# B times input for seven of sixteen states by ScalarE scales and TensorE transposes, and C rows by DMA

## The chip, the cores and the metric

One core of one Trainium2 chip runs the whole program. The metric is the device time of one execution in microseconds (us); the median of several executions is compared. A profile of one execution gives a time for every instruction; it has a span (first to last instruction) and a time of its own, which is a little longer.

## What is computed

Three layers on `x` (8 batches of 256 rows with 128 columns): half an expert layer (8 experts, the best two of each row), a Mamba block, and half an expert layer again, each with a layer norm ahead. The change is in the Mamba block:

```python
gate  = silu(x_conv) * z
delta = softplus(gate @ W_dt.T + b_dt)
BC    = gate @ W_xproj.T
B_p, C_p = (BC[..., :n], BC[..., n:])                 # n = 16 states
delta_A   = exp(einsum('bld,dn->bldn', delta, -exp(A_log)))
delta_B_x = einsum('bld,bln,bld->bldn', delta, B_p, gate)
h = a * h + bx                                        # scan over the 256 rows of a batch
y = einsum('lbdn,bln->bld', hs, C_p)
```

So for each state n: a decay, an input (delta times gate times B of the state), a scan along the rows, a product with C of the state, and a sum over the states.

## The kernel before

The 128 channels lie on the partitions. The 2048 rows are four groups of 512 (two batches each, `GT` = 512); a group runs through 16 states, so the stage has 64 states, numbered k = 16 q + n. Every engine has a queue of its own and does it strictly in order; the order is written out by hand, with semaphores between the engines.

For one state before the change:

- TensorE spreads row n of B over all partitions into PSUM bank n % 2 (`spread_b`, L965, a matmul with a one-hot column), five states ahead, and row n of C into bank 2 + n % 2 (`spread_c`, L971), four states ahead.
- ScalarE makes the decay exp(delta times -A) into PSUM bank 4 + n % 2 (`decay`, L677) one state ahead, and copies the C row into SBUF (`copy_c`, L717).
- VectorE multiplies the B row with delta times gate (`b_times_input`, L1378, the tile called `gate` holds that product by then), one state ahead of the scan, then scans (`scan`, L1385).
- POOL multiplies the scan with the C row (`step`, L507) into a ring of four, and TensorE adds the result into the PSUM bank of y with an identity matmul (`sum_states`, L981). Scan k waits for product k - 4 of POOL, which waits for sum k - 8.

Within the 16 states of group q the next group is prepared: TensorE makes the B and C product behind sum 2 (`through_w_bc`, L933) and the delta product behind sum 5 (`through_w_dt`, L937); ScalarE copies B and C at its step 5 (`bc_hi`, L636), does abs and relu of delta at steps 7 and 8, exp and log at 10 and 11 (L639 to L650); VectorE adds the low part of B and C at step 6 (`bc_lo`, L1339); POOL adds to delta behind its product 11 (`add_delta`, L487; it waits for the logarithm, `log_done`, ahead of product 11) and multiplies gate with delta behind product 12 (`gate_delta`, L491, which raises `dg_ready`). The first B product of the next group on VectorE waits for `dg_ready`. VectorE also sums y of the group before at step 2 (`y_add`, L1371).

In the last group nothing is prepared; TensorE's queue has the old rows of the next router (`old_rows`, L1042, two matmuls with 8 columns at each of states 4 to 11) and, at state 13, the y transposes and the output gate (`y_rows`, L1027, `through_out_gate`, L1048).

SP issues DMAs; between the loads of the first expert layer's rows and the stores ahead of the second expert layer it has none.

## Time and profile before

| | us |
|---|---|
| runs | 446.58, 448.4, 448.22; median 448.22 |
| the profiled execution | 445.89, span 444.1 |
| state stage, first B product to the last sum of y | 169.42 to 290.16: 120.7 |
| busy over the span: TensorE, VectorE, POOL, ScalarE | 393.5, 311.4, 279.0, 229.6 |

Times in the rows are us from the span's start. PE is TensorE, PEld its weight loads, DVE VectorE, ACT ScalarE, POOL GpSimd, SP the engine that issues DMAs. L numbers are lines of the kernel. An engine's operations overlap a little: the distance between two starts says what one costs, the length says when its result is there.

### The profile page before, as it was taken

What the parts mean: (1) busy time and instruction counts of PE and PEld (TensorE: products, weight loads), DVE (VectorE), ACT (ScalarE), POOL (GpSimd) and SP (SyncE); (2) the same over time, 40 slices, a digit from 0 to 9 for tenths busy, and PEclk for the clock granted to TensorE, in tenths of its full rate; (3) what the DMA queues carried; (4) which work ended last, traced back from release to release, by engine and by line L of the source; (5) the groups of instructions that cost most, each with busy time, mean ns of one, the idle gap of its engine ahead of it and who ended that gap; (6) DMA issues with size and microseconds to landing.
All of it is one profiled execution on the core that took longest, in us unless ns stands there. A gap on an engine that the chain in (4) does not pass through costs nothing. (4 is left out here: it accounts for less than half of the span.)

```text
span 444.1 us, 10062 instructions
## 1 busy us (share of the span) xinstructions
PE 393.5 (89%) x2636; PEld 309.0 (70%) x2637; DVE 311.4 (70%) x820; ACT 229.6 (52%) x544; POOL 279.0 (63%) x263
## 2 busy tenths in 40 slices
PE   8689999999996898989979889992799999999970
PEld 5349999999996343534334345671499999999970
DVE  4765555555557867999999999989655555555565
ACT  3635444444443248686776866534564444444410
POOL 2147777777634152788687796775477767777340
PEclk9869999999999899999999999998799999999995
DMA  7952111111230300000000000001111111112305
GB/s 255 370 184 85 52 48 45 41 53 44 45 115 6 95 0 0 1 2 0 1 0 0 0 1 1 1 1 48 66 52 48 49 41 48 47 44 45 110 22 190
DMA packets 12254, 25.05 MB, mean 56 GB/s; under 512 B 3517, under 2 KB 5060, under 8 KB 11968
## 3 DMA queue, kind: packets, MB, share of 16 engines
q1 hardware_dynamic: 7232, 15.38, 10.0%
q0 software_dynamic: 4992, 9.32, 7.7%
q8 instruction: 12, 0.20, 0.2%
q14 instruction: 18, 0.15, 0.1%
HBM read 17.34 MB, written 8.26 MB: 58 GB/s over the span
## 5 line engine op out<-in xcount | busy, mean ns | idle before, releaser
L853 PE MATMUL ps<-xT,w_now 128*128 128x128 f32 x1248 | 152.6, 275 | 0.9 <-ACT xT L590 0.7
L853 PEld LDWEIGHTS ps<-xT,w_now 128*128 128x128 f32 x1248 | 145.8, 192 | 1.8 <-ACT xT L590 1.2
L1276 DVE TENSOR_TENSOR hidden<-ps,hidden 128x256 f32<-128x256 f32 x156 | 58.9, 419 | 87.0 <-PE ps L853 87.0
L460 POOL DMA_INDIRECT expert_rows<-ysb,put_i x78 | 81.4, 1044 | 46.0 <-DVE ysb L1284 33.3
L607 ACT ACTIVATE hidden<-ps 128x256 f32<-128x256 f32 x156 | 51.4, 381 | 110.2 <-PE ps L853 110.1
L452 POOL DMA_INDIRECT xg<-xn_rows,get_i x78 | 80.5, 1032 | 41.5 <-issue 13.4
L512 POOL TENSOR_TENSOR shared<-ring_space,shared 128x512 f32<-128x512 f32 x64 | 81.7, 1289 | 32.5 <-DVE ring_space L1392 18.0
L878 PE MATMUL ps<-w_down,hidden 128*128 x624 | 81.9, 275 | 0.0
L878 PEld LDWEIGHTS ps<-w_down,hidden 128*128 128x128 f32 x624 | 75.7, 192 | 0.0
L987 PE MATMUL ps<-shared,consts 128*128 128x512 f32 x128 | 68.3, 616 | 8.0 <-POOL shared L512 7.8
L723 ACT COPY shared<-ps 128x512 f32<-128x512 f32 x64 | 37.5, 587 | 31.0 <-DVE ring_space L1392 17.8
L600 ACT COPY w_now<-w_gate_up 128x512 f32 x78 | 48.1, 620 | 7.2 <-issue 7.2
L681 ACT ACTIVATE ps<-xn,neg_a 128x510 f32<-128x510 f32 (+1 forms) x64 | 44.7, 699 | 0.2 <-DVE xn L1367 0.2
L968 PE MATMUL ps<-bc,sel_r 96*128 96x512 f32 (+1 forms) x64 | 43.6, 687 | 0.9 <-ACT xnT L546 0.8
L1392 DVE TENSOR_TENSOR_SCAN ring_space<-ps,ring_space 128x512 f32<-128x512 f32 x32 | 38.6, 1210 | 0.8 <-DVE ring_space L1382 0.8
L1392 DVE TENSOR_TENSOR_SCAN ring_space<-ps,hidden 128x512 f32<-128x512 f32 x32 | 38.3, 1205 | 0.0
L1268 DVE COPY w_now<-w_gate_up 128x512 f32 x78 | 34.8, 448 | 3.1 <-issue 2.9
L987 PEld LDWEIGHTS ps<-shared,consts 128*128 128x128 f32 x128 | 21.5, 189 | 19.6 <-POOL shared L512 16.5
L1284 DVE COPY ysb<-ps 128x128 f32<-128x128 f32 x78 | 22.7, 292 | 15.6 <-PE ps L878 8.7
L779 PE MATMUL ps<-ones_b 128*128 128x512 bf16 x84 | 27.7, 496 | 2.6 <-POOL xnT L417 1.3
L424 POOL TENSOR_TENSOR rstd<-var_e,neg_half 128x4 f32<-128x4 f32 (+1 forms) x10 | 12.1, 1206 | 28.0 <-DVE var_e L1129 28.0
L974 PE MATMUL ps<-bc,sel_r 96*128 96x512 f32 (+1 forms) x64 | 27.1, 427 | 2.8 <-ACT shared L723 2.3
(172 smaller groups left out, 397.2 us busy)
## 6 DMA issues: line engine op xcount, KB each, us to landing
w_gate_up<-in_experts SPq DMA_DIRECT2D x8, 512.0 KB, 8.2
xn_rows<-xn SPq DMA_DIRECT2D x8, 256.0 KB, 3.9
w_down<-in_experts SPq DMA_DIRECT2D x1, 2048.0 KB, 11.1
ring_space<-expert_rows SPq DMA_DIRECT2D x2, 1024.0 KB, 5.2
xg<-xn_rows,get_i POOLq DMA_INDIRECT x78, 2.6
expert_rows<-ysb,put_i POOLq DMA_INDIRECT x78, 2.3
x<-in_x_rows SPq DMA_DIRECT2D x4, 256.0 KB, 4.7
gate<-expert_rows SPq DMA_DIRECT2D x3, 256.0 KB, 3.4
```

The costliest lines, as they stand in the source:

```text
L452: pool.indirect_dma_start(out=xg[:, r, :], out_offset=None, in_=xn_dram[l], in_offset=bass.IndirectOffsetOnAxis(ap=get_i[:, t:t + 1].bitca ...
L460: pool.indirect_dma_start(out=y_dram[l], in_=ysb[:, t % RING, :], in_offset=None, out_offset=bass.IndirectOffsetOnAxis(ap=put_i[:, t:t + 1 ...
L512: pool.tensor_tensor(hc[:, n % 4, :], hs[:, n % 4, :], c_row[:, n % 4, :], ALU.mult).then_inc(hc_ready, 1)
L600: nc.scalar.copy(w_now[:, slot % W_SLOTS, 0:F], flat_gate_up[:, bass.ds(at, F)]).then_inc(w_gate_ready, 1)
L607: nc.scalar.activation(gelu[:, slot % 2, half], ps[:, GATE_BANK[slot % 2], half], ACT.Gelu).then_inc(gelu_done, 1)
L681: nc.scalar.activation(to, from_delta, ACT.Exp, scale=neg_a[:, n:n + 1]).then_inc(decay_ready, 1)
L853: m = pe.matmul(ps[:, bank, f * P:(f + 1) * P], w_now[:, slot % W_SLOTS, first + f * P:first + (f + 1) * P], xT[:, slot % X_SLOTS, :], sta ...
L878: m = pe.matmul(ps[:, RESULT_BANK[slot % 2], 0:D], hact[:, slot % H_SLOTS, f * P:(f + 1) * P], flat_down[:, bass.ds(expert + f * D, D)], s ...
L968: pe.matmul(ps[:, n % 2, :], sel_r[0:BCR, n:n + 1].to_broadcast([BCR, P]), bc[0:BCR, bass.ds(q * GT, GT)], start=True, stop=True).then_inc ...
L987: pe.matmul(y_bank(q), ident, hc[:, n % 4, :], start=(n == 0), stop=(n == N - 1)).then_inc(hc_summed, 1)
L1276: dve.tensor_tensor(hact[:, slot % H_SLOTS, half], ps[:, UP_BANK[slot % 2], half], gelu[:, slot % 2, half], ALU.mult).then_inc(hact_done, 1)
L1392: dve.tensor_tensor_scan(hs[:, n % 4, :], ps[:, DECAY_BANK + n % 2, :], bx[n % 4], 0.0, ALU.mult, ALU.add).then_inc(h_ready, 1)
```

## The change

Of the 16 states of a group, nine (`PLAIN`: 0, 1, 2, 4, 6, 8, 10, 12, 14) keep their way: spread of B, product on VectorE, decay into PSUM. But B now has one PSUM bank instead of two (`B_BANK`; state 1 of group 0 alone uses `PREP_BANK`). The other seven (`TURNED`: 3, 5, 7, 9, 11, 13, 15) go another way. Once a group TensorE transposes delta times gate (`turn_u`, behind sum 12, after `dg_ready`) and computes B with rows on the partitions (`turned_b`, behind the B and C product); ScalarE copies both to SBUF (`copy_u`, `copy_bt`). For each turned state ScalarE scales the four blocks of the turned input by the column of turned B (`scale_u`), and TensorE transposes the four results back into PSUM (`turn_scaled`), from which the scan reads them; the decay of a turned state goes to SBUF. ScalarE makes decays and scalings three states ahead instead of one (`ACT_LAG`), and TensorE turns four ahead (`TURN_LAG`).

C is no longer spread and copied by TensorE and ScalarE: ScalarE copies the last 32 of 96 rows of the B and C product to SBUF (`c_sb`), SP stores the 16 C rows of a group to HBM (`store_c`) and loads each row to all 128 partitions by a broadcast DMA into a ring of eight (`c_rows`), seven states ahead; POOL waits for the landing instead of for ScalarE.

The groups 1 and 2 were a hardware loop on each engine; on TensorE and ScalarE they are now written out. The core of the diff:

```diff
+B_LAG, TURN_LAG, ACT_LAG = 5, 4, 3
+TURNED = 3, 5, 7, 9, 11, 13, 15
+PLAIN = tuple(n for n in range(N) if n not in TURNED)
+B_BANK, PREP_BANK, S_BANK = 0, 1, 2
...
+            def c_rows():
+                store_c(0)
+                for q in range(GROUPS):
+                    sp.wait_ge(c_stored, 16 * (q + 1))
+                    for n in range(N):
+                        k = q * N + n
+                        if n == C_STORE_AT and q + 1 < GROUPS:
+                            store_c(q + 1)
...
+                        if k >= C_RING:
+                            sp.wait_ge(hc_ready, k - C_RING + 1)
+                        sp.dma_start(c_row[k % C_RING], c_dram[k:k + 1].to_broadcast([P, GT])
+                                     ).then_inc(c_loaded[k % C_RING], 16)
...
+                def scale_u(q, n):
+                    act.wait_ge(u_copied, q + 1)
+                    act.wait_ge(bt_copied, q + 1)
...
+                    for c in range(GC):
+                        i = nc.scalar.activation(scaled[:, side(n), c, :], ut[:, q % 2, c, :], ACT.Copy, scale=bt[:, q % 2, c, n:n + 1])
+                    i.then_inc(scaled_ready, 1)
+
+                def make_ready(q, n):
+                    if n in TURNED:
+                        scale_u(q, n)
+                    decay(q, n)
...
                     for n in range(N):
                         before(q, n)
-                        copy_c(q * N + n, n, False, False)
-                        decay(q + (n + 1) // N, (n + 1) % N)
+                        make_ready(q + (n + ACT_LAG) // N, (n + ACT_LAG) % N)
                         prepare(q, n)
...
+                def spread_b(q, n, bank=B_BANK):
+                    if past(plain_before(q, n)):
+                        pe.wait_ge(bx_ready, plain_before(q, n) - (bank != B_BANK))
...
+                def turn_scaled(q, n):
+                    pe.wait_ge(scaled_ready, turned_before(q, n) + 1)
...
+                    for c in range(GC):
+                        t = pe.transpose(ps[:, S_BANK + side(n), c * P:(c + 1) * P], scaled[:, side(n), c, :], ident)
+                    t.then_inc(scaled_turned, 1)
+
+                def feed(q, n):
+                    if (n + B_LAG) % N in PLAIN:
+                        spread_b(q + (n + B_LAG) // N, (n + B_LAG) % N)
+                    if (n + TURN_LAG) % N in TURNED:
+                        turn_scaled(q + (n + TURN_LAG) // N, (n + TURN_LAG) % N)
...
                         through_w_bc(q + 1, next_bank(q))
+                        pe.wait_ge(u_copied, q + 1)
+                        turned_b(q + 1, ps[:, PREP_BANK, :])
...
+                    if n == PE_U_AT:
+                        pe.wait_ge(bt_copied, q + 2)
+                        turn_u(q + 1)
...
+                    else:
+                        dve.wait_ge(scaled_turned, turned_before(q, n) + 1)
+                        dve.wait_ge(sb_decay_ready, turned_before(q, n) + 1)
+                        kept, added = sb_decay[:, side(n), :], ps[:, S_BANK + side(n), :]
```

## Rows read from the trace of the kernel before

**Rows 1.** Windows by group: stretch, length, busy by engine, PEclk, DMA share, GB/s.
```profile
169.42:200.91 31.49, 28.29 (x75) 12.99 (x73) 29.59 (x35) 24.81 (x43) 19.67 (x16) 1.00 0.00 1
200.91:229.97 29.06, 25.84 (x68) 11.75 (x68) 28.76 (x35) 21.30 (x38) 22.57 (x19) 1.00 0.00 0
229.97:259.17 29.20, 25.80 (x69) 11.75 (x68) 28.92 (x34) 21.24 (x38) 22.84 (x19) 1.00 0.00 0
259.17:290.16 30.99, 29.92 (x120) 17.78 (x120) 30.85 (x51) 18.41 (x32) 24.90 (x20) 1.00 0.00 1
```

**Rows 2.** Timeline of VectorE: start, length, engine, line, operation, tiles, count.
```profile
208.96 0.66 DVE L1382 TENSOR_TENSOR ring_space<-ps,gate 128x512 f32<-128x512 f32 x1
209.54 1.21 DVE L1392 TENSOR_TENSOR_SCAN ring_space<-ps,ring_space 128x512 f32<-128x512 f32 x1
...
212.97 0.67 DVE L1342 TENSOR_TENSOR bc<-ps,bc  x1
...
227.60 2.33 DVE L1392 TENSOR_TENSOR_SCAN ring_space<-ps,hidden 128x512 f32<-128x512 f32 x2
...
290.16 0.68 DVE L1375 TENSOR_TENSOR gate<-ps,xnT 128x512 f32<-128x512 f32 x1
```

**Rows 3.** Timeline of POOL, products 11 and 12 of group 1, with idle time before.
```profile
224.37 1.30 POOL L512 TENSOR_TENSOR shared<-ring_space,shared 128x512 f32<-128x512 f32 x1 [1.04 <-ACT hidden L650]
225.61 1.29 POOL L488 TENSOR_TENSOR xn<-xn,hidden 128x512 f32 x1
227.15 1.28 POOL L512 TENSOR_TENSOR shared<-ring_space,shared 128x512 f32<-128x512 f32 x1 [0.26 <-DVE ring_space L1392]
228.38 1.28 POOL L492 TENSOR_TENSOR gate<-gate,xn  x1
```

**Rows 4.** Timeline of ScalarE in group 1, from its step 7 to the logarithm.
```profile
216.05 0.59 ACT L723 COPY shared<-ps 128x512 f32<-128x512 f32 x1 [2.30 <-PE ps L938]
216.53 0.70 ACT L681 ACTIVATE ps<-xn,neg_a 128x510 f32 x1
217.16 0.68 ACT L640 ACTIVATE hidden<-ps,vectors 128x512 f32 x1
...
223.51 0.62 ACT L650 ACTIVATE hidden<-hidden 128x512 f32<-128x512 f32 x1
```

**Rows 5.** Timeline of ScalarE, two forms of 128 columns elsewhere in the program.
```profile
294.49 4.24 ACT L566 ACTIVATE shared<-ps,yrstd 128x128 f32<-128x128 f32 x16 [7.56 <-PE ps L1036]
...
309.16 1.65 ACT L557 ACTIVATE xn<-x,shift,rstd 128x128 f32<-128x128 f32 x4 [2.27 <-POOL shift L430]
```

**Rows 6.** Timeline of TensorE: records in a run (a float32 matmul is two records).
```profile
172.65 1.88 PE L930 MATMUL ps<-xnT,mats 128*128 128x512 f32 x4
...
203.00 1.02 PE L987 MATMUL ps<-shared,consts 128*128 128x512 f32 x2
...
204.08 0.39 PE L974 MATMUL ps<-bc,sel_r 96*128 96x512 f32 x1
204.31 1.02 PE L987 MATMUL ps<-shared,consts 128*128 128x512 f32 x2
...
285.20 1.05 PE L1031 MATMUL ps<-consts,gate 128*128 128x128 f32 x8
286.09 0.96 PE L1050 MATMUL ps<-out_gate,gate 128*128 128x8 f32 x8
```

**Rows 7.** Timeline of ScalarE ahead of group 0 and at its decay 2.
```profile
164.07 0.69 ACT L640 ACTIVATE hidden<-ps,vectors 128x512 f32<-128x512 f32 x1 [0.28 <-PE ps L938]
...
174.85 0.69 ACT L681 ACTIVATE ps<-xn,neg_a 128x510 f32<-128x510 f32 x1
```

**Rows 8.** The page: DMA rate in 40 slices; issues, count, KB, us to landing.
```profile
GB/s 255 370 184 85 52 48 45 41 53 44 45 115 6 95 0 0 1 2 0 1 0 0 0 1 1 1 1 48 66 52 48 49 41 48 47 44 45 110 22 190
...
gate<-expert_rows SPq DMA_DIRECT2D x3, 256.0 KB, 3.4
```

**Rows 9.** Windows, columns as in rows 1: a stretch ahead of the second expert layer.
```profile
305.00:310.00 5.00, 0.00 (x0) 0.00 (x0) 4.69 (x28) 2.73 (x8) 2.12 (x4) 0.65 0.28 107
```

More of the change, by code:

```diff
@@ L104, with plain_before, turned_before, side @@
 assert HEAD + LOOPS * UNROLL == NT - TAIL and UNROLL % RING == 0 and UNROLL % 6 == 0
+def plain_before(q, n):
+    return q * len(PLAIN) + sum(m < n for m in PLAIN)
+def turned_before(q, n):
+    return q * len(TURNED) + sum(m < n for m in TURNED)
+def side(n):
+    return (PLAIN.index(n) if n in PLAIN else TURNED.index(n)) % 2
+def earlier_on_side(q, n):
+    kind = PLAIN if n in PLAIN else TURNED
+    for m in range(n - 1, n - 1 - N, -1):
+        if m % N in kind and side(m % N) == side(n):
+            if m < 0 and isinstance(q, int) and q == 0:
+                return None
+            return q * N + m
 def past(value):
@@ L266, in macaron_block @@
         silu = shared[:, 4 * GT:6 * GT].rearrange("p (r t) -> p r t", r=2)
-        c_row = shared[:, 4 * GT:8 * GT].rearrange("p (r t) -> p r t", r=4)
-        bc = sb("bc", [BCR, T], F32R)
+        w_rows = w_now[:].rearrange("p s w -> p (s w)")
+        c_row = ([w_rows[:, r * GT:(r + 1) * GT] for r in range(C_RING - 2)]
+                 + [shared[:, (6 + r) * GT:(7 + r) * GT] for r in range(2)])
+        bc = sb("bc", [BC_ROWS, T], F32R)
+        c_sb = sb("c_sb", [BCR, T])
+        bt = sb("bt", [P, 2, GC, N])
+        ut = sb("ut", [P, 2, GC, D])
+        scaled = sb("scaled", [P, 2, GC, D])
+        sb_decay = sb("sb_decay", [P, 2, GT])
         soft = hidden[:, 2, :]
@@ L516, in mamba @@
                     before(0, n)
-                    step(n, n, n < 4)
+                    step(0, n, n < 4)
                     prepare(0, n)
@@ L715, in mamba @@
                 nc.scalar.preload_act_table_set("natural_log_exp_and_others")
[L717 to L725 removed]
                 decay(0, 2)
[L727 removed]
+                copy_u(0)
+                act.wait_ge(sb_decay_padded, 1)
                 for n in range(N):
                     before(0, n)
[L730 to L732 removed]
+                    make_ready((n + ACT_LAG) // N, (n + ACT_LAG) % N)
                     prepare(0, n)
[L734 removed]
+                for q in range(1, GROUPS - 1):
                     for n in range(N):
                         before(q, n)
[L737 to L738 removed]
+                        make_ready(q + (n + ACT_LAG) // N, (n + ACT_LAG) % N)
                         prepare(q, n)
[L740 to L743 removed]
+                for n in range(N - ACT_LAG):
+                    make_ready(GROUPS - 1, n + ACT_LAG)
             act_expert = [act.alloc_register(f"act_expert_{r}") for r in range(UNROLL)]
@@ L956, in mamba, with turned_b, turn_u @@
                 convolve(1)
+                def turned_b(q, bank):
+                    for c in range(GC):
+                        m = pe.matmul(bank[:, c * N:(c + 1) * N], gate[:, q * GT + c * P:q * GT + (c + 1) * P],
+                                      mats[:, M_BC:M_BC + N], start=True, stop=True)
+                    m.then_inc(bt_made, 1)
+                def turn_u(q):
+                    pe.wait_ge(dg_ready, q + 1)
+                    for c in range(GC):
+                        t = pe.transpose(ps[:, PREP_BANK, c * P:(c + 1) * P], gate[:, q * GT + c * P:q * GT + (c + 1) * P], ident)
+                    t.then_inc(u_turned, 1)
                 turn_group(1, 2)
@@ L1010, in mamba @@
                 spread_b(0, 2)
-                spread_b(0, 3)
+                pe.wait_ge(bx_ready, 2)
+                turn_u(0)
                 pe.wait_ge(silu_done, GROUPS)
-                for n in range(C_LAG):
-                    spread_c(0, n, n < 2)
-                spread_b(0, 4)
+                for n in range(3, TURN_LAG):
+                    if n in TURNED:
+                        turn_scaled(0, n)
+                for n in range(3, B_LAG):
+                    if n in PLAIN:
+                        spread_b(0, n)
                 pe.wait_ge(gate_ready, GROUPS)
@@ L1019, in mamba @@
                     prepare(0, n)
-                    spread_ahead(0, n)
-                with pe.Fori(1, GROUPS - 1) as q:
+                    feed(0, n)
+                for q in range(1, GROUPS - 1):
                     for n in range(N):
@@ L1376, in y_add, with b_times_input @@
                                       ALU.add).then_inc(yT_ready, 1)
-                def b_times_input(q, n, ring_new=False):
-                    dve.wait_ge(b_spread, q * N + n + 1)
-                    if not ring_new:
-                        dve.wait_ge(h_ready, q * N + n - 3)
-                    dve.tensor_tensor(bx[n % 4], ps[:, n % 2, :], gate[:, bass.ds(q * GT, GT)],
+                def b_times_input(q, n, bank=B_BANK):
+                    if n not in PLAIN:
+                        return
+                    dve.wait_ge(b_spread, plain_before(q, n) + 1)
+                    earlier = earlier_on_side(q, n)
+                    if earlier is not None:
+                        dve.wait_ge(h_ready, earlier + 1)
+                    dve.tensor_tensor(bx[side(n)], ps[:, bank, :], gate[:, bass.ds(q * GT, GT)],
                                       ALU.mult).then_inc(bx_ready, 1)
@@ L1399, in mamba @@
                 dve.wait_ge(dg_ready, 1)
-                b_times_input(0, 0, True)
-                b_times_input(0, 1, True)
+                b_times_input(0, 0)
+                b_times_input(0, 1, PREP_BANK)
                 scan(0, 0, True)
@@ L1405, in mamba @@
                 gate_product(3)
-                b_times_input(0, 2, True)
+                b_times_input(0, 2)
                 for n in range(2, N):
```

129 lines of the change are left out of this document (75 added, 54 removed).

## The prediction

> **What bounds the kernel now.** I read the windows view first, cut at the first B product (`b_times_input(q, 0)`) of each group and, for the end, at the last y sum on VectorE [rows 1]. The stage that the change touches is 120.7 us long: 31.5, 29.1, 29.2 and 31.0 us for groups 0 to 3. VectorE is busy in 28.8 of 29.1 us of group 1, so it is full there, and TensorE's granted clock is 1.00 (2.4 GHz) in all four. The reader should then see how VectorE spends it, in its timeline [rows 2]: a B product starts 0.58 us before the scan behind it (208.96, 209.54), two scans without a product between them start 1.12 us apart (2.33 for both, 1.21 for one). So a state costs 1.71 us, and 16 states with the low part of B and C (0.6) and the sum of y (0.6) give 28.6: with a hiccup of 0.3, the group.
>
> But VectorE isn't alone. POOL's timeline [rows 3] shows a second bound right behind the first: POOL sits 1.04 us before product 11, waiting for ScalarE's logarithm (`log_done`, L498), then does product 11, `add_delta`, product 12 and `gate_delta`, which ends at 229.66. Only then may VectorE start group 2 (`dg_ready`, L1419); it does so at 229.97. The slack is 0.3 us. The logarithm is late because ScalarE stood 2.30 us until the delta product of L938 came from TensorE [rows 4]. That chain goes through all engines and isn't VectorE's load, so a lighter VectorE doesn't shorten it by itself.
>
> **The change on VectorE and POOL.** Seven products of 16 go: 7 x 0.58 = 4.1 us a group. VectorE's floor falls to 16 x 1.13 + 9 x 0.58 + 1.2 = 24.5 us. A turned scan still has one operand in PSUM and one in SBUF (they change places), so I keep 1.13. POOL keeps its 18 operations at 1.24 to 1.29, about 23 us [rows 3].
>
> **ScalarE.** Gone: 16 copies at 0.48 (216.05 to 216.53), 7.7 us a group. New: 28 scalings of 128 columns. No row shows that exact form. Below: 0.255 us each (4.24 for 16, the last lasting about 0.41) for Copy with a scale per partition out of PSUM. Above: 0.39 (1.65 for 4) for Identity with a scale and a bias per partition out of SBUF [rows 5]. Here it is Copy, one such operand, out of SBUF: I take 0.29, nearer the first, whose function and operands it shares; four are 1.16. Also new are the copies of the turned input (0.5), of turned B (0.2) and of C (0.5). Sum: 28 x 0.29 + 1.2 - 7.7 = +1.6 us a group, from 21.3 busy: still under VectorE.
>
> **TensorE.** A float32 matmul of 512 columns is two records 0.43 apart, 0.86 ((1.88 - 0.59) / 3). A step of the loop is 1.31 (203.00 to 204.31), so each spread costs 0.23. Eight transposes take 1.05, so four cost 0.44. Eight records with 8 columns take 0.96, 0.10 each; `turned_b` (eight records with 16 columns) is 0.8 to 1.0, I take 0.9 [rows 6]. Per group: 16 + 7 spreads removed (5.3), 32 transposes (3.5) and 0.9 added. TensorE has less to do, but in another order, and its queue is strict.
>
> **The chain in the new order.** I follow one group from `dg_ready`, adding only pieces that wait for each other.
> 1. VectorE: product 0 (0.66). B has one PSUM bank now, so the spread for product 1 can't run ahead: 0.4 to 0.5 (0.39 for one record [rows 6], and two hand-overs). Product 1 (0.58), scan 0 (1.21): 3.1.
> 2. ScalarE: decay 2 waits for scan 0 (0.62), then the copy of the turned input (0.59) and the scalings for state 3 (3 x 0.29 + 0.41 = 1.28): with hand-overs 2.65.
> 3. TensorE has `turn_scaled(3)` in its queue ahead of sum 0, so sums 0 to 5 all stand behind step 2. Up to the delta product it runs without a gap: three turnings (1.3), six sums (5.2), two spreads (0.5), the B and C product (0.86), `turned_b` (0.9), the delta product (0.86), and 0.2 until its result: 9.7.
> 4. ScalarE waits for that product at step 7, then until the logarithm: five decays, abs, relu, exp and log at 0.6 to 0.63 a piece [rows 4] and two sets of scalings (2.3): 8.0.
> 5. POOL, as now: 5.2 [rows 3].
> With 0.2 of hand-overs 28.8 us. **The chain, not VectorE, sets the group.** Before it was 29.06 and 29.20, so groups 1 and 2 give 0.3 + 0.4. The stall of VectorE for the low part (it waits for ScalarE's copy, 0.8) and the wait of POOL before product 11, which grows to some 2 us, lie inside the 28.8; last scan 15 waits behind product 11 and `turn_scaled(15)`, and still ends 0.9 ahead of `dg_ready`.
>
> **Group 0.** ScalarE's abs started at once when the delta product landed [rows 7]. Now the copy of C (0.48) and of turned B stand ahead of it, the latter waiting for `turned_b`, which TensorE does after the delta product: +1.0 on everything behind. Decay 2 starts at 175.85 instead of 174.85, the copy and scalings end at 178.4, TensorE's block (9.8: one spread more) at 188.4, ScalarE 196.4, POOL 201.7: group 1 starts at 201.8 instead of 200.91, **+0.9**.
>
> **Group 3** has no preparation, but TensorE's queue holds the old rows (0.1 a record, 0.41 to 0.44 a state in eight states) and at the end the y transposes and output gate. From the group's start: 5.75 until `turn_scaled(3)`, turnings 7 x 0.44, sums 16 x 0.86, five spreads 1.2, old rows 3.5, y rows and gate 1.7, tail 0.2: 29.2 against 31.0 now (259.17 to 290.16 [rows 1, 2]), **-1.8**. VectorE's last scan would end at 24.6 and its first two statistics of y at about 27.6, so TensorE ends last here.
>
> **C by DMA.** The store (32 KB) and six loads are issued when C is copied at about 164 [rows 7], eight us before the first product can want a row; later rows are asked for seven states ahead, over 12 us. A transfer of 256 KB lands in 3.4 us, and the queue has moved 370 GB/s [rows 8]; 256 KB per 1.8 us is 146 GB/s. SP has nothing else to issue in the stage. I cost it at nothing; the cover is gone if the repeated reading of one row falls under 146 GB/s.
>
> **Sum.** +0.9 - 0.3 - 0.4 - 1.8 = -1.6 us. The profiled execution took 445.89 (span 444.1), so it would be 444.3; the median of the runs is 448.22, so I forecast **446.6**. Its own range, 443.5 to 449.5, comes from 0.255 instead of 0.29 (-0.35 a group over three) and `turned_b` on one side, hand-overs at every new semaphore and 0.12 a record for the old rows (0.96 over 8 [rows 6]) on the other.
>
> **Rivals.**
> *The chain opens, VectorE stays the bound.* If ScalarE's pieces overlap better than I add them, the next floor is VectorE's 24.5 with 0.6 for product 1 and 0.8 for the low part: 25.9 in groups 1 and 2 (-6.5), about -1.5 in group 0, -1.8 in group 3: -9.8, 438.4; halfway 442.5. For it: VectorE is the fullest engine [rows 1]. Against: `dg_ready` now comes only 0.3 ahead [rows 3].
> *Scalings at 0.39.* Three sets lie in the chain: +1.1 a group over three, 0.3 in group 3: +3.6, 450.2. Bounded by the second row of [rows 5].
> *TensorE's clock falls* (the slower side). In the new order TensorE idles 2.7 us before sum 11 and 1.5 before `dg_ready`. The clock has stood at 1.00 in this stage [rows 1], but behind idle time it fell to its half level, 1.2 GHz (0.65 as the mean of 305 to 310, TensorE without any work [rows 9]). At half clock sum 11 and `turn_scaled(15)` take 1.5 us more, 0.6 beyond their slack; a third of the block of step 3 at half clock takes 1.6 more. At 1.6 in each of three groups it is +5, 451.6, and it decides from the point at which a gap of 2.7 us is enough for the fall. The Trainium skill (TensorE: Matmul & The Clock Gate, Part 4: PE-mode transpose) says that transposes do not count as busy for the gate the way matmuls do; by that rule the 32 new transposes in place of 23 spreads make the fall likelier. No row here shows transposes alone in such a stretch.
> *C rows late.* At 120 GB/s a row takes 2.18 us, 35 us a group: +24, 470. Against: [rows 8].
>
> **Chances.** Forecast 0.46, open chain 0.22, dear scalings 0.12, clock 0.13, C late 0.05, others 0.02. A difference of 0.5% (2.2 us) is about what a measurement of this kernel can tell from none. Faster by more: 0.22 and two fifths of the forecast's range, 0.40. Within: the rest of that range, most of the dear scalings, part of the clock's, 0.39. Slower: 0.21. The range that leaves out 0.1 on each side: 440 to 452.
>
> **What would show it.** In the profile after: groups of 28 to 29.5 us with VectorE idle 2 to 4 us in each, its longest wait before product 0 for POOL's `gate_delta`; POOL waiting about 2 us for L650's logarithm before product 11; ScalarE waiting for the delta product; sum 0 directly behind four transposes; scalings at 0.29; VectorE starting group 0 about 1.0 later; clock 1.00. Groups near 26 us, or a TensorE without waits for ScalarE, would make the chain wrong; a POOL that waits for DMA would make the C step wrong.

## The result and the profile after

| | before | after |
|---|---|---|
| median of the runs, us | 447.4 | 454.71 (452.9 to 456.13) |
| ratio, 95% interval | | 1.0181 [1.0143, 1.0220] |
| the profiled execution, span | 445.89, 444.1 | 456.13, 454.3 |

The change makes the kernel 1.8% slower. I had forecast 446.6 with a range of 440 to 452. Here and below a ratio leaves out executions more than 1.5% above the fastest of the same kernel.

Behind the state stage nothing moves: from the last sum of y to the end it is 153.9 us in both profiles. The loss lies in the stage, and the stage also starts 1.9 us later. Of these 1.9, 1.0 is there before the change does anything in this block: the silu of ScalarE ahead of the copy of C (L633 before, L700 after) starts at 161.05 and 162.07. The same silu starts anywhere from 160.4 to 163.8 in the kernels that the experiments made from after, so this 1.0 is not the change's. The other 0.9 is: from the silu to the stage it is 9.27 us against 8.37.

The windows view, cut at the first B product of each group as in [rows 1] (columns: stretch, length, busy time and instructions of TensorE, its weight loads, VectorE, ScalarE and POOL, then granted clock, DMA share, GB/s), of the kernel after:

```profile
171.34:206.61 35.27, 31.07 (x94) 14.07 (x93) 25.82 (x29) 27.36 (x59) 20.22 (x16) 0.90 0.40 130
206.61:237.51 30.90, 27.23 (x87) 12.38 (x85) 24.79 (x29) 22.51 (x52) 22.83 (x19) 0.94 0.42 138
237.51:268.52 31.01, 27.26 (x82) 12.33 (x82) 24.79 (x29) 22.51 (x52) 23.01 (x19) 0.92 0.42 137
268.52:300.38 31.86, 31.23 (x129) 17.08 (x128) 27.18 (x46) 17.53 (x43) 24.95 (x21) 0.97 0.30 92
```

VectorE did get its 4 us: it is busy in 24.8 of 30.9 us of group 1, where it was busy in 28.8 of 29.1. But all four groups are longer than in [rows 1], and a second thing is new: TensorE's granted clock, 1.00 everywhere before, is 0.90 to 0.97.

The timeline of TensorE in group 1 of the kernel after (start, length, engine, line, operation, tiles, records, idle time before). L1084 is `turn_scaled`, L1099 the sums, L1075 the spread of B, L1031 the delta product:

```profile
212.51 0.66 PE L1084 MATMUL ps<-consts,scaled 128*128 128x128 f32 x4 [0.83 <-ACT scaled L779]
213.00 1.88 PE L1099 MATMUL ps<-shared,consts 128*128 128x512 f32 x4
214.81 0.50 PE L1075 MATMUL ps<-bc,sel_r 64*128 64x512 f32 x1
215.24 0.66 PE L1084 MATMUL ps<-consts,scaled 128*128 128x128 f32 x4
215.74 1.02 PE L1099 MATMUL ps<-shared,consts 128*128 128x512 f32 x2
...
221.94 1.02 PE L1031 MATMUL ps<-gate,mats 128*128 128x512 f32 x2
...
232.53 2.01 PE L1099 MATMUL ps<-shared,consts 128*128 128x512 f32 x2 [2.24 <-POOL shared L579]
234.48 0.79 PE L1075 MATMUL ps<-bc,sel_r 64*128 64x512 f32 x1
235.20 1.04 PE L1084 MATMUL ps<-consts,scaled 128*128 128x128 f32 x4
```

Two readings. First, two sums and a spread take 2.24 us (213.00 to 215.24), of which two sums are 1.72, so this spread costs 0.52, not the 0.23 that [rows 6] gave. Its record reads 64x512 where the record of before reads 96x512. Second, behind a wait of 2.24 us sum 11 (232.53) takes 2.01 instead of 1.02 and the four turnings behind it 1.04 instead of 0.66: half clock, 1.2 GHz. The windows view of 233 to 236, where the granted clock reads 0.50:

```profile
233.00:236.00 3.00, 3.00 (x7) 1.09 (x6) 0.00 (x0) 1.42 (x3) 2.75 (x3) 0.50 0.24 87
```

The end of that group, on VectorE (scan 15, then product 0 of group 2) and on POOL (product 11, `add_delta`, product 12, `gate_delta`):

```profile
236.37 1.22 DVE L1524 TENSOR_TENSOR_SCAN ring_space<-sb_decay,ps 128x512 f32<-128x512 f32 x1 [4.16 <-PE ps L1084]
237.51 0.67 DVE L1508 TENSOR_TENSOR ring_space<-ps,gate 128x512 f32<-128x512 f32 x1
...
231.18 1.30 POOL L579 TENSOR_TENSOR shared<-ring_space,w_now 128x512 f32<-128x512 f32 x1 [3.09 <-DVE ring_space L1524]
232.43 1.28 POOL L554 TENSOR_TENSOR xn<-xn,hidden 128x512 f32 x1
233.96 1.28 POOL L579 TENSOR_TENSOR shared<-ring_space,w_now 128x512 f32<-128x512 f32 x1 [0.26 <-POOL xn L554]
235.19 1.28 POOL L558 TENSOR_TENSOR gate<-gate,xn  x1
```

`gate_delta` ends at 236.47. Scan 15, held up by the turning at half clock, lets VectorE go only at 237.51: 1.04 behind it. (POOL's 3.09 are put down to VectorE, but scan 11 had ended at 228.3; the wait also holds the logarithm, which ended at 230.93.)

The rows of C come in time. The page's DMA issues, and POOL's three longest waits in the stage by their sums (what for, us in total, times, longest), of the kernel after:

```profile
w_now<-c_rows SPq DMA_DIRECT2D x48, 256.0 KB, 3.5
shared<-c_rows SPq DMA_DIRECT2D x16, 256.0 KB, 3.4
```

```profile
POOL shared L579 <- DVE ring_space L1524: 34.2, 29, 5.5
POOL shared L579 <- ACT hidden L730: 3.1, 1, 3.1
POOL shared L579 <- PE ps L1099: 2.4, 3, 1.1
```

No wait of POOL in the stage is for a DMA, among these or the others.

### The profile page after: what moved, and what is told of

It reads as the page before. It is cut to its first block, busy times and chain, and to the rows that moved or that the text cites. A ratio compares the mean times of both kernels' runs of the same rounds, so it can differ in the third digit from the quotient of the medians.

```text
span 454.3 us, 10186 instructions
## 1 busy us (share of the span) xinstructions
PE 404.2 (89%) x2704; PEld 315.3 (69%) x2705; DVE 295.5 (65%) x792; ACT 235.1 (52%) x604; POOL 277.9 (61%) x264
## 4 chain that ended last, share of the span: by engine, by line
PE 73%; DVE 8%; ACT 6%; issue 5%; DMA 4%; POOL 2%; SPq 0%; DVEq 0%; POOLq 0%; ACTq 0%
PE ps L945 31%; PE ps L970 15%; PE ps L1099 9%; PE ps L1084 3%; PE ps L1013 3%; PE ps L1075 2%; ACT scaled L779 2%; PE ps L940 2%; DMA xg<-xn_rows,get_i 1%; POOL shared L579 1%; DVE stats L1245 1%; DVE ring_space L1524 1%; DMA expert_rows<-ysb,put_i 1%; PE ps L882 1%; PE ps L871 1%
## 5 line engine op out<-in xcount | busy, mean ns | idle before, releaser
L945 PEld LDWEIGHTS ps<-xT,w_now 128*128 128x128 f32 x1248 | 147.3, 194 | 1.5 <-ACT xT L657 1.1
L526 POOL DMA_INDIRECT expert_rows<-ysb,put_i x78 | 79.4, 1018 | 46.9 <-DVE ysb L1407 29.2
L579 POOL TENSOR_TENSOR shared<-ring_space,w_now 128x512 f32<-128x512 f32 x48 | 61.8, 1299 | 32.8 <-DVE ring_space L1524 26.6
L1099 PE MATMUL ps<-shared,consts 128*128 128x512 f32 x128 | 69.3, 648 | 6.5 <-POOL shared L579 6.5
L1524 DVE TENSOR_TENSOR_SCAN ring_space<-ps,ring_space 128x512 f32<-128x512 f32 x36 | 42.8, 1197 | 0.0
L1524 DVE TENSOR_TENSOR_SCAN ring_space<-sb_decay,ps 128x512 f32<-128x512 f32 x28 | 33.8, 1206 | 13.3 <-PE ps L1084 13.3
L768 ACT ACTIVATE ps<-xn,neg_a 128x510 f32<-128x510 f32 x36 | 24.4, 680 | 27.6 <-DVE ring_space L1524 17.6
L779 ACT ACTIVATE scaled<-ut,bt 128x128 f32<-128x128 f32 x112 | 35.5, 388 | 0.8 <-PE ps L1084 0.6
L1099 PEld LDWEIGHTS ps<-shared,consts 128*128 128x128 f32 x128 | 21.7, 200 | 20.4 <-POOL shared L579 11.9
L1508 DVE TENSOR_TENSOR ring_space<-ps,gate 128x512 f32<-128x512 f32 x36 | 24.1, 671 | 6.9 <-PE ps L1075 6.7
L1075 PEld LDWEIGHTS ps<-bc,sel_r 64*128 64x128 f32 x36 | 7.0, 196 | 28.9 <-issue 19.6
```

What stands on the lines that cost most here:

```text
L526: pool.indirect_dma_start(out=y_dram[l], in_=ysb[:, t % RING, :], in_offset=None, out_offset=bass.IndirectOffsetOnAxis(ap=put_i[:, t:t + 1 ...
L579: pool.tensor_tensor(hc[:, n % 4, :], hs[:, n % 4, :], c_row[n % C_RING], ALU.mult).then_inc(hc_ready, 1)
L779: i = nc.scalar.activation(scaled[:, side(n), c, :], ut[:, q % 2, c, :], ACT.Copy, scale=bt[:, q % 2, c, n:n + 1])
L945: m = pe.matmul(ps[:, bank, f * P:(f + 1) * P], w_now[:, slot % W_SLOTS, first + f * P:first + (f + 1) * P], xT[:, slot % X_SLOTS, :], sta ...
L1099: pe.matmul(y_bank(q), ident, hc[:, n % 4, :], start=(n == 0), stop=(n == N - 1)).then_inc(hc_summed, 1)
L1524: dve.tensor_tensor_scan(hs[:, n % 4, :], kept, added, 0.0, ALU.mult, ALU.add).then_inc(h_ready, 1)
```

## The experiments

Four theories stood after this reading. The clock: TensorE at half speed behind its waits. The chain through all engines as forecast, which POOL's order (products 11 and 12 behind the logarithm) makes long. The C rows by DMA. And, after the run with C alone, the 64 rows of the spread. The table is the windows view of each profiled execution, cut as above; the ratio is to the kernel before, with its 95% interval. The kernel before ran again beside each set of runs, with medians of 447.4 beside after, 447.1 beside e1 to e4, 445.84 beside e5 to e8 and 447.54 beside e9 to e12; so compare ratios between rows rather than medians.

| kernel | group 0 | 1 | 2 | 3 | stage | median | ratio |
|---|---|---|---|---|---|---|---|
| before | 31.49 | 29.06 | 29.20 | 30.99 | 120.7 | | |
| after | 35.27 | 30.90 | 31.01 | 31.86 | 129.0 | 454.71 | 1.0181 [1.0143, 1.0220] |
| e1_clock | 32.56 | 30.22 | 30.18 | 31.17 | 124.1 | 452.54 | 1.0101 [1.0056, 1.0147] |
| e2_pool | 32.00 | 27.60 | 27.60 | 31.13 | 118.3 | 445.93 | 0.9984 [0.9948, 1.0019] |
| e3_c_only | 33.94 | 28.60 | 30.06 | 33.33 | 125.9 | 450.02 | 1.0071 [1.0037, 1.0104] |
| e4_late | 33.29 | 29.31 | 29.30 | 31.19 | 123.1 | 451.87 | 1.0111 [1.0057, 1.0166] |
| e5_all | 30.49 | 27.58 | 27.60 | 31.15 | 116.8 | 444.74 | 0.9977 [0.9949, 1.0005] |
| e6_before_pool | 31.50 | 28.94 | 30.16 | 31.71 | 122.3 | 447.91 | 1.0048 [1.0023, 1.0073] |
| e7_rows96 | 31.94 | 29.50 | 29.50 | 29.83 | 120.8 | 447.95 | 1.0051 [1.0019, 1.0083] |
| e8_c_rows96 | 30.29 | 28.60 | 28.59 | 31.09 | 118.6 | 445.07 | 0.9978 [0.9956, 1.0001] |
| e10_rows_clock | 31.18 | 29.52 | 29.51 | 29.85 | 120.1 | 446.75 | 0.9997 [0.9950, 1.0044] |
| e9_best | 28.86 | 27.29 | 27.32 | 29.84 | 113.3 | 440.46 | 0.9857 [0.9815, 0.9900] |
| e12_rows_pool | 29.07 | 27.27 | 27.29 | 29.83 | 113.5 | 439.94 | 0.9841 [0.9802, 0.9880] |

**The clock (e1_clock).** bf16 matmuls of ones into a free bank, `keep_clock`, which the kernel already has elsewhere, fill TensorE's waits (`CLOCK_AT` is 11):

```diff
+                    if n == CLOCK_AT and q < GROUPS - 1:
+                        pe.wait_ge(dt_read, q + 2)
+                        keep_clock(8, 7 - (q + 1) % 2)
                     pe.wait_ge(hc_ready, k + 1)
...
                 pe.wait_ge(silu_done, GROUPS)
+                pe.wait_ge(gate_ready, GROUPS - 1)
+                keep_clock(8, 6)
                 for n in range(3, TURN_LAG):
```

> The changed kernel with eight plain matmuls of 512 columns (bf16, into a PSUM bank that nobody reads) in TensorE's queue ahead of the first turn_scaled of group 0 and ahead of sum 11 of groups 0 to 2, where it idles over 2 us. Theory clock: what the prediction missed is mostly the half clock behind these gaps (sum 11 took 2.01 us instead of 1.02 to 1.12, and turn_scaled(15), for which scan 15 waits, comes behind it). Then groups 1 and 2 fall from 30.9 to 29.9 us, group 0 from 35.3 to about 33, the granted clock is 1.00 in the stage, and the time goes from 454.7 to about 450. Rival, the chain alone (the half clock falls into slack): no change, 454 to 456.

The clock is 1.00 in all four groups and the stage 4.9 us shorter, 0.8 points of the ratio. So the half clock was real and paid for, but it is not, as I had expected here, most of what the prediction missed: with full clock the kernel is still 1% slower than before (452.54, not 450), and groups 1 and 2 still take 30.2. In place of the late scan VectorE now waits 0.78 for POOL's `gate_delta`.

**POOL's order (e2_pool).** Product 12 no longer stands behind the logarithm, nor product 11:

```diff
-                    if n == POOL_DELTA_AT:
-                        pool.wait_ge(log_done, q + 2)
-                    if n == POOL_GATE_AT:
-                        pool.wait_ge(delta_ready, q + 2)
+                    pass
...
-                    if n == POOL_DELTA_AT:
-                        add_delta(q + 1)
                     if n == POOL_GATE_AT:
+                        pool.wait_ge(log_done, q + 2)
+                        add_delta(q + 1)
+                        pool.wait_ge(delta_ready, q + 2)
                         gate_delta(q + 1)
```

> The changed kernel with POOL's wait for the logarithm moved from ahead of product 11 to behind product 12, and add_delta and gate_delta next to each other there. Theory chain: the group is set by logarithm, two products, add_delta, gate_delta (5.5 us from the logarithm to dg_ready, of which two products are 2.5), and sum 11 with turn_scaled(15) stands behind product 11. With the products ahead of the wait dg_ready comes 2.6 us behind the logarithm, TensorE has no gap ahead of sum 11, and groups 1 and 2 go from 30.9 to about 27.5 us; time 445. Rival, another engine is next at once (ScalarE or TensorE full): groups stay over 30 us, time 453 or more.

Groups 1 and 2 fall from 31 to 27.60. POOL's timeline in this kernel: products 11 and 12 (x2), then at once what the next group needs:

```profile
224.26 2.54 POOL L577 TENSOR_TENSOR shared<-ring_space,w_now 128x512 f32<-128x512 f32 x2 [0.29 <-DVE ring_space L1522]
227.05 1.27 POOL L554 TENSOR_TENSOR xn<-xn,hidden 128x512 f32 x1 [0.25 <-ACT hidden L728]
228.48 1.28 POOL L558 TENSOR_TENSOR gate<-gate,xn  x1 [0.16 <-POOL xn L554]
```

The wait of 3.09 ahead of product 11 is gone, and with it TensorE's wait ahead of sum 11: the granted clock is 1.00 in groups 1 to 3 without any filler. One order on POOL made the chain long and, in groups 1 and 2, the clock low. Group 0 still reads 0.95: there the wait is another, 2.12 us ahead of the first turning.

**The same order before the change (e6_before_pool)**, as a control:

> A control: the kernel before with the POOL order that took 3.3 us a group off the kernel after (add_delta and gate_delta both behind product 12). VectorE is busy in 28.8 of 29.1 us there, so by the theory that VectorE sets the groups before and the chain sets them after, the order gives at most 0.3 us a group: 446 to 447.5. If POOL's wait for the logarithm set the kernel before too, its groups get over 1 us shorter, and it is 444 or less.

447.91, ratio 1.0048 [1.0023, 1.0073]; the stage takes 122.3 against 120.7. No gain, rather a small loss. The windows of its groups 1 and 2 (columns as above):

```profile
200.67:229.61 28.94, 25.98 (x68) 11.58 (x68) 28.67 (x36) 21.18 (x38) 22.81 (x19) 1.00 0.00 0
229.61:259.77 30.16, 27.16 (x68) 12.60 (x68) 28.89 (x35) 21.09 (x38) 22.87 (x19) 0.94 0.00 0
```

Group 1, at full clock, takes 28.94 against 29.06 before: VectorE sets the group there (28.67 of 28.94 busy), so the order is worth 0.1. In the profiled execution the loss is the clock's: with this order TensorE waits 2.22 us for POOL where group 1 goes over into group 2, and 2.24 at the next such place, where it had waited 1.17 at most, and groups 2 and 3 read 0.94 and 0.95 and take 30.16 and 31.71. So here the same order brings the half clock that it removes in the kernel after. It is worth 3.3 us a group only behind the change, where the chain and not VectorE sets the group.

**C by DMA alone (e3_c_only).** The kernel before with `store_c` and `c_rows` instead of `spread_c` and `copy_c`; B as before, except that its spread, as in the kernel after, contracts over 64 rows:

> One part of the change alone: the kernel before with C rows by DMA from HBM, B as before for all sixteen states (loops of TensorE and ScalarE written out as in the change). Theory: the C part costs nothing in the groups, VectorE stays full at 28.6 to 29.1 us a group, POOL never waits for a landing, and the whole cost of the change comes from the turned B; time 447 to 448.5, with ScalarE some 7 us a group less busy. Rival, the transfers or their landing cost: groups over 29.5 us or POOL with DMA as the releaser of its waits, time over 450.

450.02, ratio 1.0071 [1.0037, 1.0104]: slower, which neither theory had. POOL never waits for a DMA here either. The windows of groups 1 and 2:

```profile
206.40:235.00 28.60, 25.90 (x52) 8.38 (x52) 28.60 (x36) 14.20 (x22) 22.82 (x19) 1.00 0.50 148
235.00:265.06 30.06, 27.85 (x51) 8.71 (x51) 28.88 (x35) 14.21 (x22) 22.88 (x19) 0.91 0.46 141
```

Group 1, at full clock, is VectorE's, as the theory had it (28.60 of 28.60 busy). The loss lies in the other three, where the clock reads 0.90 to 0.93. There TensorE, which does less than before, is the late one. Its timeline while it catches up, at full clock again (L1003 sums, L991 spreads):

```profile
241.05 0.50 PE L991 MATMUL ps<-bc,sel_r 64*128 64x512 f32 x1
241.48 1.13 PE L1003 MATMUL ps<-shared,consts 128*128 128x512 f32 x2
242.53 0.49 PE L991 MATMUL ps<-bc,sel_r 64*128 64x512 f32 x1
```

A sum and one spread take 1.48 (241.05 to 242.53). In [rows 6] a sum and two spreads took 1.31. So one spread of 64 rows costs 0.62 where two of 96 rows cost 0.45. A state of VectorE is 1.71, so a TensorE that has fallen behind makes up only 0.2 a state.

**96 rows (e7_rows96, e8_c_rows96).** B needs 64 rows; the third set of 32 meets zeros in the selector, so it can be contracted over without harm:

```diff
-        bc = sb("bc", [BC_ROWS, T], F32R)
+        bc = sb("bc", [BCR, T], F32R)
...
-                    nc.scalar.copy(bc[0:BC_ROWS, group_cols(q)], bank[0:BC_ROWS]).then_inc(bc_hi_done, 1)
+                    nc.scalar.copy(bc[:, group_cols(q)], bank[0:BCR]).then_inc(bc_hi_done, 1)
...
-                    pe.matmul(ps[:, bank, :], sel_r[0:BC_ROWS, n:n + 1].to_broadcast([BC_ROWS, P]),
-                              bc[0:BC_ROWS, bass.ds(q * GT, GT)], start=True, stop=True).then_inc(b_spread, 1)
+                    pe.matmul(ps[:, bank, :], sel_r[0:BCR, n:n + 1].to_broadcast([BCR, P]),
+                              bc[0:BCR, bass.ds(q * GT, GT)], start=True, stop=True).then_inc(b_spread, 1)
```

> The kernel after with one difference: the spread of a B row contracts over 96 rows again, as before, and not over 64 (the third set of rows has zeros in the selector, so the sums are the same). Theory (the 64 row operand is the mis-sized step): a sum with a spread behind it takes 1.48 us of TensorE in the changed kernel, where the kernel before fitted a sum and two spreads into 1.32; if the 64 rows cost the switch, sum and spread take 1.09 here, nine times a group. Between the scalings of state 3 and the delta product stand two of them, so groups 1 and 2 get 0.8 shorter (about 30.0), group 0 too, group 3, where TensorE sets the pace, 2 to 3 us shorter (about 29); total 449 to 451. Rival (a single spread between sums is dear whatever its rows, and the second spread shared the price before): pitch 1.48 and 454 to 456 as before this edit. The half clock behind the wait before sum 11 stays in either case.

> The kernel with only the C rows by DMA (B as in the kernel before), with spreads over 96 rows and not 64. By the theory of the 64 rows the state's sum and spread fall from 1.48 to 1.09 us and the loss of that kernel against the kernel before (450.0 against 447.1) goes: 446 to 448, groups of 28.6 to 29. By the rival (a lone spread is dear) nothing changes: 449 to 451. If the loss was only TensorE's half clock after an idle stretch, lighter sums make the idle time longer, and it is 450 or more.

Both go the way of the theory, and further than I expected (447.95 for 449 to 451, 445.07 for 446 to 448). The loss of after falls from 1.81% to 0.51%, and the stage from 129.0 to 120.8. Part of it is the clock, which I thought would stay: it reads 0.95, 0.94, 1.00 and 1.00 in the four groups of e7_rows96, 0.90 to 0.97 in those of after. C alone goes from 450.02 to 445.07 (ratio 0.9978 [0.9956, 1.0001]), with groups 1 and 2 at 28.6 to 28.8 from one sum of y to the next and a clock of 0.97 or more in every group. TensorE in group 1 of e7_rows96:

```profile
208.56 1.88 PE L1099 MATMUL ps<-shared,consts 128*128 128x512 f32 x4
209.88 0.80 PE L1075 MATMUL ps<-bc,sel_r 96*128 96x512 f32 x1
210.51 0.61 PE L1084 MATMUL ps<-consts,scaled 128*128 128x128 f32 x4
210.95 1.02 PE L1099 MATMUL ps<-shared,consts 128*128 128x512 f32 x2
```

Two sums and a spread take 1.95 (208.56 to 210.51), the spread 0.23; the turning behind it 0.44. Both are the prediction's own figures. The weight loads (PEld) show where the difference goes, first of after, then of e7_rows96; the bracket is the time since the load before it:

```profile
213.87 0.19 PEld L1099 LDWEIGHTS ps<-shared,consts 128*128 128x128 f32 x1 [0.24 <-issue]
214.81 0.18 PEld L1075 LDWEIGHTS ps<-bc,sel_r 64*128 64x128 f32 x1 [0.76 <-DVE ring_space L1508]
```

```profile
209.43 0.19 PEld L1099 LDWEIGHTS ps<-shared,consts 128*128 128x128 f32 x1 [0.24 <-issue]
209.85 0.19 PEld L1075 LDWEIGHTS ps<-bc,sel_r 96*128 96x128 f32 x1 [0.24 <-DVE ring_space L1508]
```

With 96 rows the spread's weights are loaded at 209.85, 0.24 after the load before ended, while the sums (208.56 and 1.88 long) still run. With 64 rows they are loaded only at 214.81, 0.76 after it, when the sums (213.00 and 1.88 long) are all but through. The Trainium skill (TensorEngine Tiling (Array Packing), Tiling Modes) says that changing the tiling mode of the array drains TensorE, and lists modes of 64 rows. The trace agrees with that, if an operand of 64 rows runs in such a mode: 0.52 to 0.62 for a spread where one of 96 rows costs 0.23. No run here shows the mode itself.

**64 rows before the change (e11_before_64rows).** The price alone, on the kernel before; both spreads with `sel_r[0:64]` and `bc[0:64]`, TensorE's loop written out:

> The kernel before with one difference: both spreads of a state contract over 64 rows and not 96 (the rows left out meet zeros in the selector). This shows the price of the 64 rows alone. TensorE fits a sum and two spreads into 1.32 us before. If each spread of 64 rows costs 0.3 more, a step takes 1.9 and TensorE 16 x 0.6 = 9.6 us a group more, 35 against the group's 29.1: it becomes the bound, 465 or more. If the price falls once per run of spreads (on the way in and out), a step takes 1.65 to 1.7, TensorE 31 to 32 a group: 452 to 458. If the rows cost nothing: 447.

The four runs are 458.04, 461.34, 469.27 and 493.29 (median 465.31); the ratio, from the first two, is 1.0282 [1.0209, 1.0354]. The times lie between and beyond the cases of the expectation and do not tell them apart; the step does. The profiled execution is the one of 469.27, whose clock reads 0.76 in group 0 and 1.00 behind it, so I read groups 1 and 2. They take 31.27 and 31.61, against 29.06 and 29.20. One step there:

```profile
222.26 0.39 PE L975 MATMUL ps<-bc,sel_r 64*128 64x512 f32 x1
222.58 1.13 PE L988 MATMUL ps<-shared,consts 128*128 128x512 f32 x2
223.63 0.50 PE L969 MATMUL ps<-bc,sel_r 64*128 64x512 f32 x1
223.97 0.39 PE L975 MATMUL ps<-bc,sel_r 64*128 64x512 f32 x1
```

The step is 1.71 (222.26 to 223.97) against 1.31: 0.40 more for two spreads in a row, as one spread alone cost 0.39 more (0.62 - 0.23). The price falls once per run of 64-row matmuls, the second of the three cases expected. It also bears on e3_c_only: C's spreads had gone, the price had come, and TensorE had little left with which to catch up once the clock had fallen.

**Full clock and 96 rows (e10_rows_clock):**

> The kernel after with spreads over 96 rows and the keep-clock matmuls of the first run (8 ahead of the first turning of group 0, 8 ahead of sum 11 of groups 0 to 2). The clock should read 1.00 in all groups. Against 96 rows alone (447.95): if the half clock in groups 0 and 1 (0.95 and 0.94 there) still costs, 1.5 in group 0 and 0.5 in group 1, 445.5 to 446.5; if with the lighter spreads the last scan has slack again, no change, 447 to 448.5.

Group 0 in the windows view:

```profile
170.06:201.24 31.18, 29.16 (x106) 14.29 (x104) 25.69 (x28) 27.17 (x59) 19.17 (x16) 1.00 0.44 144
```

Groups 0 and 1 of e7_rows96, without the keep-clock matmuls:

```profile
170.23:202.17 31.94, 27.24 (x94) 14.07 (x92) 25.61 (x28) 27.16 (x59) 19.86 (x16) 0.95 0.44 144
202.17:231.67 29.50, 24.69 (x83) 12.34 (x82) 24.88 (x29) 22.51 (x52) 22.53 (x19) 0.94 0.42 143
```

The clock reads 1.00 in all four groups here. Beside e7_rows96 only group 0 moves (31.94 to 31.18). In group 1 of e7_rows96 the clock read 0.94 and the group took 29.50 all the same: with lighter spreads the last scan has its slack back. The half clock cost 4.9 us of the stage beside the 64 rows and 0.7 without them. The median, 446.75, lies between the cases of the expectation's numbers and doesn't tell them apart; the windows do.

**turned_b later (e4_late).** `turned_b` moved behind the delta product, out of the chain:

```diff
-                        pe.wait_ge(u_copied, q + 1)
-                        turned_b(q + 1, ps[:, PREP_BANK, :])
...
                         through_w_dt(q + 1, next_bank(q))
+                        pe.wait_ge(u_copied, q + 1)
+                        turned_b(q + 1, ps[:, PREP_BANK, :])
```

> The changed kernel with turned_b moved on TensorE's queue from behind the B and C product to behind the delta product. Theory chain: the 0.8 us of turned_b lies between scan 0 and the logarithm, so each of groups 0 to 2 gets 0.8 shorter: 30.9 to 30.1 in groups 1 and 2, time 452.3. Rival, the group is set by scan 15 and the clock behind the gap and not by the length of TensorE's block: no change in the groups, 454.7.

Groups 1 and 2 get 1.6 to 1.7 shorter. Against e1_clock, where the clock is 1.00 too, it is 0.9 (30.22 to 29.31), close to what `turned_b` takes (0.80 from its start to the next sum, 0.96 to the end of its eight records). In all it is twice the 0.8 that I expected. The other 0.7 is the clock's, by the same comparison: the wait ahead of sum 11 was 1.44 here, and the sum behind it took 1.13.

**Putting the mends together (e5_all, e9_best, e12_rows_pool).** e5_all is e2_pool with e4_late and keep-clock matmuls (four ahead of sum 11):

> The kernel after with all three mends of the runs before this one: add_delta and gate_delta both behind product 12 on POOL, turned_b behind the delta product, and keep-clock matmuls (8 ahead of the first turning of group 0, 4 ahead of sum 11 of groups 0 to 2). If the theory of the chain and that of the clock add up: groups 1 and 2 at 26.8 (27.6 less 0.8 for turned_b), group 0 at 30.5, group 3 at 31.1 as TensorE's queue sets it; 442 to 443. If another bound stands right behind (the last scan behind product 15 and turn_scaled(15), or VectorE), groups stay at 27.6 and the time at 445 to 446.

A miss in groups 1 and 2: 27.58, not 26.8. The last turning is late again, this time behind the fillers themselves (L870) and the sum that they hold up:

```profile
227.00 1.03 PE L870 MATMUL ps<-ones_b 128*128 128x512 bf16 x4
...
229.25 0.66 PE L1083 MATMUL ps<-consts,scaled 128*128 128x128 f32 x4
...
230.03 1.22 DVE L1528 TENSOR_TENSOR_SCAN ring_space<-sb_decay,ps 128x512 f32<-128x512 f32 x1 [0.85 <-PE ps L1083]
```

> The kernel after with spreads over 96 rows, add_delta and gate_delta both behind product 12 on POOL, turned_b behind the delta product, and 8 keep-clock matmuls ahead of the first turning of group 0 only (those ahead of sum 11 held the last turning up by 0.85 us a group in the run that had them with the POOL order). If the three causes add up: groups 1 and 2 at 27.6 - 0.8 - 0.6 = 26.2, near VectorE's floor of 25.9; group 0 at 30, group 3 at 29.8 as with 96 rows alone; stage 112 to 113 against 120.7 before, total 438 to 440. If TensorE, with less to do, falls to half clock at a wait in groups 1 and 2, groups are 27.5 or more and the total 441 to 443.

> The kernel after with two mends only: spreads over 96 rows, and add_delta and gate_delta both behind product 12. Against the run above it lacks turned_b behind the delta product and the keep-clock matmuls. If those still cost what they did (0.8 a group over three, and some 1.5 in group 0): 441 to 443. If the causes overlap, so that the POOL order and the 96 rows remove the same stall, 444 to 446.

e12_rows_pool has two mends, the 96 rows and POOL's order, and e9_best adds the later `turned_b` and eight fillers ahead of group 0. Both are at 440 and both beat the kernel before, by 1.6% and 1.4%, with intervals that overlap: the two further mends add nothing (groups of 27.3 in both, 1.1 over what I expected of e9_best), and e12_rows_pool is faster than either case that I had written down for it. C by DMA alone does not give this: e8_c_rows96 stands at 0.9978, and VectorE is busy in all 28.6 us of its groups 1 and 2. Below that a group gets only with a lighter VectorE, which is what the turned states bring. e12_rows_pool in the windows view, group 1:

```profile
198.70:225.97 27.27, 24.39 (x87) 11.89 (x88) 24.87 (x29) 22.54 (x53) 23.03 (x19) 1.00 0.50 157
```

The clock is 1.00 in all four groups. What ends the group now shows on POOL: `add_delta` follows product 12 without a wait (222.96), and product 0 of group 2 then waits 0.40 for `gate_delta`:

```profile
220.44 2.56 POOL L577 TENSOR_TENSOR shared<-ring_space,w_now 128x512 f32<-128x512 f32 x2 [0.26 <-DVE ring_space L1522]
222.96 1.26 POOL L554 TENSOR_TENSOR xn<-xn,hidden 128x512 f32 x1
224.39 1.27 POOL L558 TENSOR_TENSOR gate<-gate,xn  x1 [0.16 <-POOL xn L554]
```

The logarithm is in time now, and the next bound is POOL's own queue behind scan 12. So a shorter chain ahead of the logarithm has nothing left to give. The 0.40 is only part of the 1.4 over the 25.9 of the rival with the open chain: VectorE is also busy for 24.9 where I had 24.5, and waits 0.81 for the spread of product 1 and 1.10 for the low part where I had 0.6 and 0.8.

## Why the prediction was wrong

The median was missed by 8.1 us (454.71 for 446.6). The account needs a trace, and the profiled execution, the longest of the four of after, took 456.13 where the sum said 444.3, 11.8 us more: the stage starts 0.9 later than I had it, and the groups are 3.9, 2.1, 2.2 and 2.7 longer than my 31.4 (201.8 less a start at 170.4), 28.8, 28.8 and 29.2. The runs divide that:

| us | group 0 | 1 | 2 | 3 | sum |
|---|---|---|---|---|---|
| half clock (after less e1_clock) | 2.7 | 0.7 | 0.8 | 0.7 | 4.9 |
| 64 rows (e1_clock less e10_rows_clock) | 1.4 | 0.7 | 0.7 | 1.3 | 4.1 |
| the rest (e10_rows_clock less forecast) | -0.2 | 0.7 | 0.7 | 0.6 | 1.8 |
| start of the stage | | | | | 0.9 |

The start is chance: 1.0 was there ahead of the change, and the change's own delay was 0.9 where I had 1.0. In another order the shares of the first two rows differ (64 rows first: 8.3 of the stage, then 0.7 for the clock); the two feed each other. The sum is the same. With the rows alone put back the median is 447.95, inside my range; with the clock alone put back it is 452.54, outside.

**The step that failed: "each spread costs 0.23" (TensorE).** I took it from a step of the loop before, whose spreads contract over 96 rows, and carried it to spreads of 64 rows, though [rows 6] gives the form of the spread, 96x512, and the edit makes it 64x512. It is 0.52 between sums and a turning, and the turning behind it 0.50 instead of 0.44. The block of step 3 of the chain holds two of them and took 10.45 (212.51 to 222.96). In e7_rows96, with the rows restored, the same block takes 9.76 (208.07 to 217.83), where I had 9.7. In group 3, whose spreads I put at the same price, the rows cost 1.3.

**The rival that came true: TensorE's clock falls, 0.13.** Its mechanism is in the trace as I wrote it: a wait ahead of sum 11 (2.24, I had 2.7), the sum and the turning at half clock, scan 15 late. I had put its price at 1.6 in each of three groups; 2.7, 0.7 and 0.8 came, and 0.7 in group 3. The 2.7 has a second place that the rival did not name: in group 0 the clock fell behind the wait ahead of the first turning, within the block of step 3 (0.50 from 181.5 to 184.5). It deserved more: the step that gave scan 15 a slack of 0.9 held only at full clock, and the full clock of [rows 1] belongs to a TensorE whose waits for POOL were 1.17 us at most. With the spreads' price on top, 451.6 becomes some 455.7 (4.1 more), and 454.71 was measured; that they come so close is in part chance, as 455.7 leaves out the rest of 1.8. The rule on transposes that I cited beside it is not what decided: e12_rows_pool, without any filler, has the same 28 turnings a group at a granted clock of 1.00, and in after the clock fell behind waits (2.12 ahead of the first turning of group 0, 2.24 ahead of sum 11).

**Right: the chain sets the group.** Its other pieces came out. Step 1 took 3.3 (3.1 forecast, though its own terms add up to only 2.9; the wait for the spread of product 1 was 0.81 and not 0.4 to 0.5). Two more sums of mine are off by 0.1 and 0.2, which decides nothing: the terms of step 3 give 9.8, and 178.4 with 9.8 gives 188.2. The scalings lie 0.29 apart (four and the next start take 1.18, 211.18 to 212.36), and step 2 took 2.6 (2.65). ScalarE's part:

```profile
223.00 0.69 ACT L768 ACTIVATE ps<-xn,neg_a 128x510 f32<-128x510 f32 x1 [1.54 <-PE ps L1031]
...
230.32 0.61 ACT L730 ACTIVATE hidden<-hidden 128x512 f32<-128x512 f32 x1
```

From the delta product (222.96) to the logarithm's end (230.93) it is 8.0 (8.0). POOL's is 5.3 (5.2). `dg_ready` came 29.86 after the group's start, against 28.8: 0.7 of the difference is the 64 rows, the rest 0.2 in step 1 and hand-overs of up to 0.3. e2_pool then cuts the chain at its last piece, and the group falls by 3.3.

**Right: C rows at no cost, dear scalings and late C excluded.** 256 KB landed in 3.5, one about every 1.9 us, and POOL waited for none. **Right with the wrong consequence: group 3 is TensorE's.** It is, and at 96 rows it falls to 29.83, 0.6 over the 29.2 forecast.

**Missed altogether: that the new order had a mend.** I wrote POOL's order down as step 5, "as now", and its longer wait before product 11 as harmless because it lay inside the chain. It was the chain: 31.0 to 27.6.

## What to carry to other kernels

When an edit changes the shape of an operand, price the instruction by a row of the new shape, and if there is none, treat its cost as unknown: here going from 96 to 64 rows, less work on paper, made each spread cost more than twice as much, and putting unused rows back in was worth 1.3% of the program. When the fullest engine is made lighter, write out the next bound in each queue's own order first; the change gained clearly only once two small operations of POOL were moved as well (e7_rows96 stands at 1.0051, e12_rows_pool at 0.9841), and the move alone gained nothing (e6_before_pool). A wait that lies "inside" a chain can still be what another engine idles on, and TensorE may then do the work behind it at half clock.

## What the hardware showed

- A matmul of 64 rows between matmuls of 128 rows costs 0.39 us more than one of 96 rows (1.48 for a sum and a spread; 1.09 would be 0.86 + 0.23), and two in a row cost the same 0.40 more together (1.71 against 1.31): the weights of the first are loaded only when the matmul before is all but through.
- The length of a wait alone does not tell whether the clock falls. Ahead of sum 11 TensorE waited 2.24 us in after and worked at half clock behind it (2.01 for a sum). In e7_rows96 it waited 2.30 in group 1, and the records behind are long (1.24 for a spread, 1.06 for a turning), and 2.30 in group 2, where they are not (0.80 and 0.60). It waited 2.35 ahead of the first turning of e12_rows_pool and kept 1.00; in e9_best it fell to 0.50 behind waits of 1.34 and 0.29 at the start of group 2. What sets these apart stays open.
- A half clock is paid for only where it meets the path: group 2 of e9_best, at 0.94, took 27.32, and group 2 of e12_rows_pool, at 1.00, took 27.29.
- Reading one row of 2 KB from HBM into all 128 partitions, 64 times in all, ran at 130 to 163 GB/s in groups 0 to 2 beside four busy engines, and nothing waited for it.
